# Issuing TensorE's row-spreading products twice in the edge stage of a graph layer

## The chip, the cores and the metric

The kernel runs on one core of a Trainium2 chip. The metric is device time in microseconds (us), from the first to the last instruction of one launch with what lies around it; lower is better.

## The reference

One hybrid graph layer on 3125 nodes of width 256 with 50000 edges: a typed attention over the edges, a linear-attention mixer and a gated feed-forward on half of the rows. The change touches only the first. Cut to what matters:

```python
K, Q, V = type_proj(xn, node_types, Wk/Wq/Wv)         # [3125, 8 heads, 32]
Ks, Qt, Vs = K[src], Q[tgt], V[src]                   # 50000 edges
for t in range(3):                                    # edge types
    scores = sum((Ks @ Wa[t]) * Qt, -1) / sqrt(32) * relation_pri[t]
    w = softmax(where(edge_type == t, scores, -inf), over all edges)
    msgs += where(edge_type == t, w * (Vs @ Wm[t]), 0)
agg = segment_sum(msgs, tgt)                          # edges are sorted by tgt
```

## The kernel before

A first stage projects keys, values and queries per node into DRAM tables. The second stage, which the change touches, walks over the edges. Edges are sorted by target; 128 x 4 of them are a **group** g (98 groups), and two groups are a **block** b (49 blocks). What follows is a third stage: the sums of the windows are joined, normalised and run through the feed-forward.

For a group, GpSimd issues four indirect DMAs that gather key and value rows by source (`rows_of`, L1415) into one of 7 slots (6 toward the end), and SyncE loads a window of 64 query rows for each half (`q_window`). The target rows are not gathered. ScalarE builds a transposed one-hot matrix `ohT` from the targets' keys (L1477, L1480), and TensorE spreads the window's rows to the edges with it (`target_rows`, L1615): for k in 0, 1 and for each half hg of the partitions one fp32 product of 64x128 with 64x256 into `qr_ps[g % 2]`, a buffer of two PSUM banks. Only the last product signals `qd`. The trace shows two matmul records for each fp32 product, so 8 records for a group. The products of a group wait until VectorE has read the same buffer two groups earlier (`at_least(pe, pr, g - 1)`).

VectorE multiplies the gathered keys by the spread rows (`products`, L1784) and sums them per head (`head_sums`, L1791); per block it subtracts a maximum (L1825), sums exponentials (L1832), adds the type mask (L1800), takes maxima (L1810), receives the turned maxima from TensorE (`maximum`, L1817) and weighs the gathered values (`messages`, L1841). TensorE sums the messages by target (`window_sums`, L1632), turns the sums (L1643), sums the exponentials (`totals`, L1653) and turns and spreads maxima (L1662, L1669). ScalarE copies (L1515, L1521), exponentiates (L1505) and builds the second one-hot matrix (L1492, L1496).

25 tiles of the mixer run in the same stage, two in every three blocks from block 7 to block 44: `mix_h` (L1685) on TensorE in the tile's block, a Gelu on ScalarE (L1537, with a table load), and in the next block `mix_y` (L1692, L1694) on TensorE and `mix_row` (L1927), statistics and gain on VectorE. So the blocks from 7 on come in threes: with `mix_h` alone (7, 10, ... 43), with both (8, 11, ... 41), with `mix_y` alone (9, 12, ... 42, and 44). In the blocks without `mix_y`, VectorE does two steps of a search for shared nodes instead (L1868 to L1885).

Every engine's order is written out by hand, and an engine works its queue strictly in that order. TensorE's order in block b is: `target_rows(2b+2)`, `turn_sums(2b-4)`, `mix_y` if any, `turn_sums(2b-3)`, `target_rows(2b+3)`, `totals(b-1)`, `mix_h` if any, `turn_maxima(b)`, `window_sums(2b-2)`, `spread_maxima(b)`, `window_sums(2b-1)`. VectorE's is: `products(2b)`, `head_sums(2b)`, `subtract(b-1)`, `products(2b+1)`, `mix_row` or a search step, `head_sums(2b+1)`, `weights(b-1)`, `mark(b)`, `maxima(b)`, `messages(2b-2)`, `maximum(b)`, `messages(2b-1)`, then the mixer's gain or a search step.

Of the kernel before, what the change touches and what calls it, by code (L numbers as in the profile page):

```python
# [95 lines left out]
def build(nc, a, out):  # L96
# [15 lines left out]
    with ExitStack() as ctx:  # L112
# [322 lines left out]
        def at_least(eng, event, count):  # L435
            if count > 0:
                eng.wait_ge(event, count)
# [58 lines left out]
        with nc.Block() as block:  # L496
# [862 lines left out]
            def in_range(g):  # L1359
                return 0 <= g < NG  # L1360
# [244 lines left out]
            def _(pe):  # L1605
                def target_rows(g):
                    if not in_range(g):
                        return
                    s = g % QRING
                    pe.wait_ge(oh, g + 1)  # L1610
                    pe.wait_ge(qin[s], 32 * (g // QRING + 1))
                    at_least(pe, pr, g - 1)
                    for k in range(2):
                        for hg in range(2):
                            ins = pe.matmul(qr_ps[g % 2][:, (2 * hg + k) * D:(2 * hg + k + 1) * D],  # L1615
                                            ohT[64 * hg:64 * hg + 64, g % 2, k * P:(k + 1) * P],
                                            qwin[64 * hg:64 * hg + 64, s, :], start=True, stop=True)
                    ins.then_inc(qd, 1)
# [80 lines left out]
                pe.wait_ge(s_end, 2)  # L1699
                pe.wait_ge(s_ed, 1)  # L1700
                target_rows(0)
                target_rows(1)
                for b in range(NB):
                    if b == SEARCH_AT - 2:
                        turn_bases(1)
                    target_rows(2 * b + 2)
                    turn_sums(2 * b - 4)
                    for m in mix_tiles(b, 1):
                        mix_y(m)
                    turn_sums(2 * b - 3)  # L1710
                    target_rows(2 * b + 3)
                    totals(b - 1)
                    for m in mix_tiles(b, 0):
                        mix_h(m)
                    turn_maxima(b)
                    if b < NB - 1:
                        window_sums(2 * b - 2)
                    spread_maxima(b)
                    if b < NB - 1:
                        window_sums(2 * b - 1)  # L1720
# [1044 lines left out]
```

## Time and profile before

| | us |
|---|---|
| median of 3 runs | 998.99 |
| lowest, highest | 997.55, 1001.36 |
| profiled execution, its own time | 997.39 |
| its span, first to last instruction | 995.6 |
| TensorE busy | 852.8 (86%) |
| VectorE busy | 781.2 (78%) |
| ScalarE busy | 607.7 (61%) |
| GpSimd busy | 597.5 (60%) |
| mean granted TensorE clock | 0.925 of full |

The shares are means over three stages with different limits. The edge stage lies between about 250 and 754 us of the span, and only there does the change act. The profile gives the stage's instructions by line; a busy time joins overlapping records, while "mean ns" is that of one record.

### The profile page before, as it was taken

How to read it: one execution, taken by the hardware profiler on the slowest of the kernel's cores; microseconds unless marked ns; L12 is line 12 of the kernel's file. 1: busy time of each engine (PE TensorE's matmuls, PEld its weight loads, DVE VectorE, ACT ScalarE, POOL GpSimd, SP SyncE). 2: the span in 40 equal slices, each digit the busy share in tenths (PEclk: the TensorE clock that was granted, in tenths of full speed). 3: DMA queues.
4: the chain of work that ended last, by engine and by line, in shares of the span. 5: the costliest groups of instructions: out<-in, count | busy, mean ns of one | idle time of the engine just before them, and what ended most of it. 6: DMA issues, size and time to landing. Idle time of an engine off the chain costs nothing.

```text
span 995.6 us, 18441 instructions
## 1 busy us (share of the span) xinstructions
PE 852.8 (86%) x5153; PEld 628.8 (63%) x5153; DVE 781.2 (78%) x1682; ACT 607.7 (61%) x1540; POOL 597.5 (60%) x745
## 2 busy tenths in 40 slices
PE   4999999995787878778888887888769989999998
PEld 3776777763454555455555555554438978888886
DVE  6855666761698999999999999999997886997542
ACT  2565676763475988888988889888753233332121
POOL 4704777776777777777777777776770245663000
PEclk9999999998587999999988889888879999999999
DMA  8922666666888888888888888887844833320012
GB/s 281 284 88 100 229 222 215 223 217 203 270 252 254 255 269 272 273 271 259 265 269 264 270 267 264 263 266 242 244 141 154 242 122 112 93 80 22 0 56 74
DMA packets 126204, 202.76 MB, mean 204 GB/s; under 512 B 19755, under 2 KB 94846, under 8 KB 126102
## 3 DMA queue, kind: packets, MB, share of 16 engines
q0 software_dynamic: 38992, 129.87, 40.6%
q1 hardware_dynamic: 76630, 61.86, 20.5%
q10 hardware_dynamic: 10480, 9.83, 3.0%
q8 instruction: 44, 0.72, 0.3%
q14 instruction: 58, 0.48, 0.2%
HBM read 160.50 MB, written 40.99 MB: 202 GB/s over the span
## 4 chain that ended last, share of the span: by engine, by line
PE 51%; DVE 13%; POOL 12%; ACT 12%; issue 9%; DMA 3%; DVEq 0%; ACTq 0%; SPq 0%; POOLq 0%
POOL big L1415 11%; PE ps L2455 9%; PE ps L2441 9%; PE ps L932 5%; PE ps L1632 4%; PE ps L1615 3%; ACT edge L1492 3%; DVE big L1841 3%; PE ps L2405 3%; PE ps L973 3%; PE ps L944 2%; PE ps L920 2%; ACT L1537 2%; DMA big<-kv_scratch,src_i 2%; DVE big L1784 2%
## 5 line engine op out<-in xcount | busy, mean ns | idle before, releaser
L1415 POOL DMA_INDIRECT big<-kv_scratch,src_i x392 | 371.9, 949 | 124.6 <-issue 116.7
L1615 PE MATMUL ps<-edge 64*128 64x256 f32 x784 | 130.9, 459 | 53.7 <-DVE big L1784 19.5
L1632 PE MATMUL ps<-big,edge 128*64 128x256 f32 x784 | 134.7, 475 | 34.7 <-DVE big L1841 34.5
L1615 PEld LDWEIGHTS ps<-edge 64*128 64x128 f32 x784 | 80.6, 216 | 95.1 <-issue 54.7
L1784 DVE TENSOR_TENSOR big<-big,ps 128x1024 f32<-128x1024 f32 x98 | 119.1, 1215 | 8.4 <-DMA big<-kv_scratch,src_i 6.6
L1791 DVE TENSOR_REDUCE ps<-big 128x32 f32<-128x1024 f32 x98 | 120.1, 1225 | 2.5
L1841 DVE TENSOR_TENSOR big<-big,ps 128x1024 f32<-128x1024 f32 x98 | 118.0, 1205 | 0.0
L1492 ACT ACTIVATE edge<-edge 128x64 f32<-128x64 f32 x392 | 103.8, 339 | 1.6
L1632 PEld LDWEIGHTS ps<-big,edge 128*64 128x64 f32 x784 | 56.7, 162 | 68.0 <-DVE big L1841 44.3
L2368 ACT ACTIVATE big<-ps,fb 128x256 f32<-128x256 f32 (+2 forms) x104 | 39.4, 461 | 87.9 <-PE ps L2441 87.9
L2455 PE MATMUL ps<-big 128*128 128x256 f32 (+1 forms) x400 | 90.2, 381 | 1.1 <-ACT big L2368 1.1
L2441 PE MATMUL ps<-big 128*128 128x256 f32 (+2 forms) x416 | 89.9, 373 | 0.6 <-ACT big L2355 0.6
L2441 PEld LDWEIGHTS ps<-big 128*128 128x128 f32 x416 | 76.1, 196 | 8.9 <-issue 0.8
L2455 PEld LDWEIGHTS ps<-big 128*128 128x128 f32 (+1 forms) x400 | 74.0, 188 | 11.9 <-issue 1.6
L1515 ACT ACTIVATE edge<-ps 128x256 f32<-128x256 f32 x98 | 35.6, 376 | 57.9 <-PE ps L1632 56.2
L1477 ACT ACTIVATE edge<-edge,iota_n 128x256 f32<-128x256 bf16 x98 | 49.0, 500 | 13.5 <-DMA edge<-key_scratch 13.2
L932 PE MATMUL ps<-big,edge 128*128 x120 | 57.2, 599 | 0.0
L1480 ACT ACTIVATE edge<-edge,ones 128x256 f32<-128x256 f32 x98 | 49.8, 508 | 10.5 <-PE ps L1615 1.7
L1496 ACT ACTIVATE edge<-edge,ones 128x256 f32<-128x256 f32 x98 | 49.8, 509 | 9.1 <-ACT edge L1492 0.4
L664 POOL DMA_INDIRECT edge<-xn_scratch,big x30 | 30.0, 1001 | 39.9 <-DMA xn_scratch<-big 24.0
L1228 DVE TENSOR_TENSOR edge<-ps,big 128x512 f32<-128x512 f32 x30 | 20.8, 692 | 36.3 <-PE ps L932 34.6
L2405 PE MATMUL ps<-bd_m,big 128*126 128x128 f32 (+1 forms) x396 | 45.1, 275 | 2.5 <-DVE big L2119 2.2
(348 smaller groups left out, 1730.5 us busy)
## 6 DMA issues: line engine op xcount, KB each, us to landing
edge<-q_scratch SPq DMA_DIRECT2D x196, 64.0 KB
big<-kv_scratch,src_i POOLq DMA_INDIRECT x392
edge<-key_scratch SPq DMA_DIRECT2D x98, 64.0 KB
agg_scratch<-big SPq DMA_DIRECT2D x16, 252.0 KB
xn_scratch<-big ACTq DMA_DIRECT2D x5, 640.0 KB, 4.2
mix_scratch<-big SPq DMA_DIRECT2D x25, 128.0 KB
mix_x_scratch<-big SPq DMA_DIRECT2D x25, 128.0 KB, 1.9
wmix<-mix_x_scratch ACTq DMA_DIRECT2D x25, 128.0 KB
```

Of the source, the lines that this page charges most:

```text
L932: ins = pe.matmul(ps[1][:, :], xgT[:, t.k, ch * P:(ch + 1) * P], wall[:, ds(ty, 1), ch, 0:2 * D].rearrange("p a o -> p (a o)"), start=(ch ...
L1415: pool.indirect_dma_start(kv_slots[s][:, k, :], None, kv_d[0:N, :], bass.IndirectOffsetOnAxis(ap=src_i[:, e:e + 1], axis=0)).then_inc(got[ ...
L1480: act.activation(ohT[:, g % 2, :], dist, ACT.Relu, bias=ones[:, 0:1], scale=-1.0).then_inc(oh, 1)
L1492: ins = act.activation(gap[:, 2 * k + hg, :], iota_m, ACT.Abs, bias=neg_key[:, e:e + 1])
L1615: ins = pe.matmul(qr_ps[g % 2][:, (2 * hg + k) * D:(2 * hg + k + 1) * D], ohT[64 * hg:64 * hg + 64, g % 2, k * P:(k + 1) * P], qwin[64 * h ...
L1632: ins = pe.matmul(sums_of(g)[64 * hg:64 * hg + 64, :], oneh[:, g % OHRING, k, hg * 64:hg * 64 + 64], kv_slots[s][:, 2 * hg + k, D:2 * D], ...
L1784: dve.tensor_tensor(k_rows, k_rows, qr_ps[g % 2].rearrange("p (k d) -> p k d", d=D), ALU.mult).then_inc(pr, 1)
L1791: dve.tensor_reduce(scr[:, g // 2 % 2, :].rearrange("p (h k) -> p k h", k=BT)[:, (g % 2) * EG:(g % 2 + 1) * EG, :], kv_slots[slot_of(g)][: ...
L1841: dve.tensor_tensor(v, v, wgt[:, g // 2 % 2, (g % 2) * EG * H:(g % 2 + 1) * EG * H] .rearrange("p (k h d) -> p k h d", h=H, d=1).to_broadc ...
L2405: ins = pe.matmul(ps[4 + ck % 4][0:n, ch * P:(ch + 1) * P], stg[k % 2][:, ch, t, at:at + n], bd_m[:, t, :], start=(t == 0), stop=(t == ETY ...
L2441: ins = pe.matmul(hslot[q % 2][:, j * GT * P:j * GT * P + w], fw1[:, ch, f * P:(f + 1) * P], cols[:, ch, at:at + w], start=(ch == 0), stop ...
L2455: ins = pe.matmul(ps[4 + t % 2][0:m, 0:D], fh[:, p % 2, f, at:at + m], fw2[:, f, :], start=(f == 0), stop=(f == FJ - 1))
```

## The change

In `target_rows`, the loop over k runs over `[0, 1]` once for groups 0 and 1, and over `[0, 1, 0, 1]` for the groups from 2 on. The second pass issues the same four products again with the same operands, into the same places of the same buffer; each starts a new sum, so the result is that of the first pass. `qd` is signalled by the last product of the second pass.

```diff
@@ target_rows(g)
                     at_least(pe, pr, g - 1)
-                    for k in range(2):
+                    for k in [0, 1] * (2 if g > 1 else 1):
                         for hg in range(2):
                             ins = pe.matmul(qr_ps[g % 2][:, (2 * hg + k) * D:(2 * hg + k + 1) * D],
                                             ohT[64 * hg:64 * hg + 64, g % 2, k * P:(k + 1) * P],
```

## Rows read from the trace of the kernel before

**Rows 1.** The page's costliest group: busy, mean ns | idle before it, its releaser.

```profile
L1415 POOL DMA_INDIRECT big<-kv_scratch,src_i x392 | 371.9, 949 | 124.6 <-issue 116.7
```

**Rows 2.** Busy by stretch: length; PE, PEld, DVE, ACT, POOL; clock, DMA share, GB/s.

```profile
350.00:400.00 50.00, 40.46 (x279) 26.84 (x279) 47.99 (x78) 43.84 (x110) 37.81 (x41) 0.97 0.86 268
...
534.74:565.32 30.58, 25.22 (x163) 16.23 (x163) 28.31 (x45) 26.12 (x65) 23.09 (x25) 0.89 0.86 264
```

**Rows 3.** Timeline of VectorE, blocks 28 to 30: start, us, what, idle before.

```profile
532.10 1.22 DVE L1784 TENSOR_TENSOR big<-big,ps 128x1024 f32<-128x1024 f32 x1
...
535.27 0.35 DVE L1825 TENSOR_TENSOR edge<-edge,ps 128x192 f32<-128x192 f32 x1 [0.69 <-ACT edge L1515]
535.54 1.21 DVE L1784 TENSOR_TENSOR big<-big,ps 128x1024 f32<-128x1024 f32 x1
...
540.36 0.27 DVE L1817 TENSOR_REDUCE mall<-ps 24x1 f32<-24x128 f32 x1
...
542.13 1.22 DVE L1784 TENSOR_TENSOR big<-big,ps 128x1024 f32<-128x1024 f32 x1
...
546.88 0.42 DVE L1927 TENSOR_TENSOR wmix<-ps,v_L_mix_b 128x256 f32<-128x256 f32 x1 [0.77 <-PE ps L1694]
...
550.63 0.27 DVE L1817 TENSOR_REDUCE mall<-ps 24x1 f32<-24x128 f32 x1
...
552.56 1.21 DVE L1784 TENSOR_TENSOR big<-big,ps 128x1024 f32<-128x1024 f32 x1
...
557.00 0.43 DVE L1927 TENSOR_TENSOR wmix<-ps,v_L_mix_b 128x256 f32<-128x256 f32 x1 [0.53 <-PE ps L1694]
...
562.68 1.22 DVE L1784 TENSOR_TENSOR big<-big,ps 128x1024 f32<-128x1024 f32 x1
```

**Rows 4.** Timeline of TensorE, blocks 29 and 30.

```profile
544.02 1.14 PE L1615 MATMUL ps<-edge 64*128 64x256 f32 x8 [1.11 <-ACT edge L1480]
545.09 0.44 PE L1643 MATMUL ps<-ident,edge 128*128 128x128 f32 x2
...
546.99 1.14 PE L1615 MATMUL ps<-edge 64*128 64x256 f32 x8
...
548.41 1.14 PE L1685 MATMUL ps<-wmix 128*128 128x128 f32 x8
549.63 0.33 PE L1662 MATMUL ps<-ident,edge 128*128 128x128 f32 x1
550.76 1.08 PE L1632 MATMUL ps<-big,edge 128*64 128x256 f32 x8 [0.80 <-DVE big L1841]
...
554.15 1.13 PE L1615 MATMUL ps<-edge 64*128 64x256 f32 x8 [0.96 <-ACT edge L1480]
...
560.89 1.98 PE L1632 MATMUL ps<-big,edge 128*64 128x256 f32 x8 [0.80 <-DVE big L1841]
...
565.25 2.08 PE L1615 MATMUL ps<-edge 64*128 64x256 f32 x8
```

**Rows 5.** Timeline of ScalarE: two table loads for the Gelu, blocks 28 and 29.

```profile
541.06 1.28 ACT L1537 ACT_TABLE_LOAD   x1
...
551.18 1.28 ACT L1537 ACT_TABLE_LOAD   x1
```

**Rows 6.** The chain that ended last: start, us, what.

```profile
342.09 1.22 DVE big L1784
...
343.45 1.14 PE ps L1615 x8
```

**Rows 7.** Timeline of VectorE: the same instruction in blocks 7 and 45.

```profile
329.99 0.27 DVE L1817 TENSOR_REDUCE mall<-ps 24x1 f32<-24x128 f32 x1
...
714.19 0.27 DVE L1817 TENSOR_REDUCE mall<-ps 24x1 f32<-24x128 f32 x1
```

**Rows 8.** Timeline of VectorE: waits for gathered rows, in blocks 6 and 22.

```profile
314.27 1.22 DVE L1784 TENSOR_TENSOR big<-big,ps 128x1024 f32<-128x1024 f32 x1 [2.34 <-DMA big<-kv_scratch,src_i]
...
474.44 1.22 DVE L1784 TENSOR_TENSOR big<-big,ps 128x1024 f32<-128x1024 f32 x1 [0.25 <-DMA big<-kv_scratch,src_i]
```

**Rows 9.** Timeline of both engines: the first turned maxima, in block 0.

```profile
262.40 0.47 PE L1662 MATMUL ps<-ident,edge 128*128 128x128 f32 x1
...
262.91 0.28 DVE L1817 TENSOR_REDUCE mall<-ps 24x1 f32<-24x128 f32 x1 [4.71 <-PE ps L1662]
```

## The prediction

> **What bounds the kernel now.** I read the page first, to see which engines are dear and where. GpSimd's gathers are its costliest group and almost never wait for another engine [rows 1]; the shares of the table show TensorE and VectorE fullest. The change acts on the edge stage alone, so the second view is busy time by stretch [rows 2]. In a stretch of the first half (350 to 400 us) VectorE is busy 47.99 of 50 us and the clock is 0.97; GpSimd gets through 41 gathers, one in 1.22 us, so 8 of them pace a block at 9.76 us. Over three blocks of the second half (30.58 us, 10.19 each) VectorE is busy 28.31, ScalarE 26.12, TensorE 25.22, and the clock is 0.89. No engine is full, yet VectorE is nearly so: its idle time, 2.27 us in three blocks, is what a change can add to or take from. The third view is the timeline of VectorE over these blocks, 28 to 30, which are the three kinds: with `mix_h` alone (call it A), with both (B), with `mix_y` alone (C) [rows 3]. It shows idle time of 0.69 us in A, behind ScalarE's copy, and of 0.77 and 0.53 us in B and C, where `mix_row` (L1927) waits for `mix_y`, which TensorE has queued behind the products of L1615. The timeline of TensorE [rows 4] shows how it comes to that, and what a low clock costs: `window_sums` takes 1.98 us at the end of C and 1.08 in B, the spreading 2.08 us after it and 1.14 elsewhere, levels of 1.2 and 2.4 GHz. The last view is ScalarE's: from one table load to the next 10.12 us [rows 5], a block of the kinds A and B filled with its work.
>
> VectorE's last view: it waits for gathered rows 2.34 us in block 6 and, for the last time among the mixer's blocks, 0.25 us in block 22 [rows 8]. So up to about there the gathers pace the stage (9.8 a block), later the chain over VectorE, TensorE and ScalarE does (10.2).
>
> **The change, part by part.** It removes nothing and moves nothing; it adds 4 products, so 8 matmul records and 8 weight loads, to each of 96 groups. The first pass of 8 starts at 544.02 and the next operation at 545.09 [rows 4], so a second pass costs 1.07 us of TensorE at the high clock; at the low one 2.08 is the record's length, about 2.0 start to start. That is 2.14 us a block, 103 us in all if nothing hid it. No transfer, copy or wait is added. The buffer is free already, since nobody reads it before `qd`, which the second pass delays.
>
> What lies behind the delay depends on the block. I take each block from the start of `products(2b)` (p) to the start of `products(2b+2)`. Where VectorE decides, the spreading starts 1.36 us after p [rows 6]; call that S.
>
> In **B** TensorE does the first spreading, a turn, then `mix_y`. Now `mix_row` starts at 546.88, 2.86 us after S at 544.02 [rows 3, 4], and it is already the one waited for. With a second pass it starts at S + 3.93 = p + 5.29. From there to the next p VectorE has 5.68 us of unbroken work (546.88 to 552.56), which gives 10.97. Then TensorE: the second spreading starts at S + 2.97 now, at S + 4.04 then, and lasts 2.14; `totals` and `mix_h` took 1.42 - 1.07 = 0.35 and 1.07 us (546.99, 548.41 and the 1.14 of L1685 less the overlap of 0.07) [rows 4]. So the maxima are turned at S + 7.60, and known 0.38 later (a record of 0.33 and a hand-over of 0.05; at the low clock the pair is 0.51 apart [rows 9]), at p + 9.34. VectorE is ready for them 3.75 us after `mix_row` (546.88 to 550.63), at p + 9.04. That adds 0.30: B takes 11.27.
>
> In **C** there is no `mix_h`, so the maxima are turned in time: 10.97. (With one pass the same sum gives 2.86 + 5.68 + 1.36 = 9.90, near the 9.76 of the gathers: the two paces lie close together now.)
>
> In **A** no `mix_y` stands between. VectorE's own work from p to p is 542.13 - 532.10 - 0.69 = 9.34. The second spreading waits for `products(2b+1)`, which starts at p + 2.75 (535.54 less 532.10 less 0.69), so it starts at p + 4.11, lasts 2.14, and with the same 1.42 and 0.38 the maxima are known at p + 8.05. VectorE is ready at p + 7.57 (540.36 less 532.10 less 0.69). A takes 9.34 + 0.48 = 9.82. The first copy hides here behind VectorE's own work.
>
> The three sum to 32.06, against 30.58. This holds at the high clock throughout; TensorE would be busy some 28 of 32 us. I take the high clock, because the clock now falls at the end of C, after `mix_h` is missing and TensorE has stood idle in several pieces, and those pieces are just what the second passes fill. ScalarE doesn't come to bind: its 10.12 us fit in A plus B (21.1) and B, and with no table loads C leaves it several us.
>
> From block 7 to block 45 there are 38 blocks, 13 of kind A, 12 of B and 13 of C (44 counted there): 13 x 9.82 + 12 x 11.27 + 13 x 10.97 = 405.5 us. They take 714.19 - 329.99 = 384.2 us now [rows 7]. That is +21.3. It is more than 12.7 times 1.48, since the first half runs at the gathers' 9.8 us and loses that cover.
>
> Before block 7: in block 0 VectorE waits 4.71 us for the maxima behind two spreadings at the low clock [rows 9], and two second passes put up to 4 us there. Behind it stands the wait of 2.34 us for rows in block 6 [rows 8], which uses up part of that. I take +1, with bounds of 0 and +2. Past block 45 no `mix_y` stands between; the copies hide as in A, and a `window_sums` at the high clock is shorter by 1.98 - 1.08 = 0.90 [rows 4]: -1 for one such in four blocks, as an estimate. Sum: +21.
>
> The profiled execution took 997.39 (span 995.6), the median of the runs is 998.99. So the execution would read about 1018, the median 1020.
>
> **A rule that speaks against this.** The rows show the clock low after a C and high after two busier blocks. The Trainium skill, TensorE: Matmul & The Clock Gate, section "HAM oscillation — how this bites in real kernels", says that pauses between bursts of matmuls send the clock to half speed again and again, and that a kernel gains by keeping TensorE busy. By that rule the second passes would be a means to gain. The fall of the clock to half agrees with the trace (1.98 against 1.08 us). The rival below prices it from rows.
>
> **The rivals.**
> *The clock pays for the copies: faster.* If the products kept the clock high and cost nothing on the path, blocks 23 to 44 would go at the gathers' 9.76 us for 10.19: 22 x 0.43 = 9.5 us less, 990. It decides if the second pass costs under about 0.3 us in front of `mix_row`: B and C then take 10.97 - 0.77 = 10.20, A 9.34, and the 38 blocks 376 us, 8 less than now. For it speaks the clock of 0.89 [rows 2]; against it that `mix_row` waits for TensorE even in the blocks at the high clock [rows 3], and that two such waits of 1.31 us (p + 5.29 against VectorE ready at p + 3.98, which is 546.88 - 0.77 - 542.13) exceed all of the 2.27 us that VectorE idles now.
> *The copies are half hidden: no change.* If the records of a second pass overlapped those of the first, at 0.5 us a pass B and C would take 10.4, A 9.3: 381 us, 3 less than now, and 995. Nothing in the rows shows two such passes back to back cheaper than their sum.
> *The clock still falls at the end of each C.* Then A starts with two passes at the low clock, 4 us for 2.14, the second spreading starts 1.9 us later than counted, and A takes about 11.9. That is 2.1 x 13 = 27 more, 1047. For it: the clock falls now exactly there.
> *TensorE becomes the bound in every block*, 2.14 us on each of 48: 1102. Against it: idle time of 1.11 and 0.80 us within a block [rows 4].
>
> **How the numbers follow.** The likeliest case, slower by the waits in B and C, has 0.80; the clock still falling 0.08; TensorE the bound 0.01; half hidden 0.06; faster by the clock 0.05. A measurement of this kernel tells about 0.5%, 5 us. Slower 0.88 (part of the half-hidden case falls there too, and part of the first in the middle), same 0.07, faster 0.05. The range: below, without the turned maxima's 0.30 and 0.48 (-10) and with 0 before block 7, less 2 for a shorter second pass, 1007; above, a clock that falls in about half of the C blocks, or ScalarE late by 0.4 us in each block, 1034.
>
> **What would show it.** L1927's idle time of 0.77 and 0.53 us should grow to about 1.3 in B and C, released by `mix_y` (L1694); L1817 should show new waits of 0.3 to 0.5 us for L1662; the three blocks should take about 32.1; the clock in the edge stage should be near 1.0 and the waits for gathered rows after block 7 gone. L1615 should have 1552 records. The prediction is wrong if the clock stays at 0.89, if L1927's wait doesn't grow, or if blocks of kind A go past 10 us.

## The result and the profile after

The changed kernel takes 1005.96 us (median of 4 runs, 1003.36 to 1006.22), the kernel before 998.49 beside it: ratio 1.0065, 95% interval 1.0037 to 1.0094. Timed a second time, on another occasion, the ratio was 1.0049 (1.0026 to 1.0073). It is slower, as forecast, but by 7 us and not by 21; the stated range began at 1007.

Of the page of the changed kernel, the costliest group of TensorE and that of the window sums:

```profile
span 1004.2 us, 19977 instructions
...
L1615 PE MATMUL ps<-edge 64*128 64x256 f32 x1552 | 199.1, 396 | 49.9 <-DVE big L1784 25.3
...
L1632 PE MATMUL ps<-big,edge 128*64 128x256 f32 x784 | 113.2, 412 | 21.4 <-DVE big L1841 20.5
```

The window sums on the page of the kernel before:

```profile
L1632 PE MATMUL ps<-big,edge 128*64 128x256 f32 x784 | 134.7, 475 | 34.7 <-DVE big L1841 34.5
```

The span grew by 8.6 us (995.6 to 1004.2). L1615 has twice its records but for two groups (784 to 1552). Nothing in `window_sums` was changed, yet its mean record takes 412 ns where it took 475: more of them run at the high clock.

Busy time of the stretch from block 7 to the place where block 45 stood before, 384 us, first the kernel before, then the changed one:

```profile
330.00:714.00 384.00, 311.74 (x2026) 202.85 (x2026) 358.20 (x572) 328.85 (x820) 287.07 (x304) 0.91 0.85 263
```

```profile
330.00:714.00 384.00, 339.97 (x2583) 249.51 (x2583) 348.71 (x559) 327.85 (x805) 281.69 (x298) 1.00 0.84 259
```

TensorE is busy 28 us more, VectorE gets through 559 instructions where it had done 572, and the granted clock is 1.00 where it was 0.91. Who VectorE waits for in this stretch, before and after (us in total, times, longest):

```profile
DVE wmix L1927 <- PE ps L1694: 11.4, 21, 0.8
DVE edge L1825 <- ACT edge L1515: 7.1, 12, 0.7
DVE big L1784 <- DMA big<-kv_scratch,src_i: 3.0, 7, 1.0
```

```profile
DVE wmix L1927 <- PE ps L1694: 30.6, 25, 1.4
DVE mall L1817 <- PE ps L1662: 0.9, 1, 0.9
```

These rows account for VectorE's idle time in the stretch: they sum to 21.5 us before and 31.5 after, and VectorE is busy 9.5 us less. `mix_row` waits 19.2 us more for `mix_y`. In return the wait of `subtract` behind ScalarE's copy (7.1 us), which came from window sums at the low clock, is gone, and so is that for gathered rows (3.0).

The timeline of VectorE over three blocks of the changed kernel, of the kinds B, C and A, to be laid beside [rows 3]:

```profile
549.68 1.22 DVE L1784 TENSOR_TENSOR big<-big,ps 128x1024 f32<-128x1024 f32 x1
...
554.76 0.42 DVE L1927 TENSOR_TENSOR wmix<-ps,v_L_mix_b 128x256 f32<-128x256 f32 x1 [1.21 <-PE ps L1694]
...
558.51 0.27 DVE L1817 TENSOR_REDUCE mall<-ps 24x1 f32<-24x128 f32 x1
...
560.44 1.21 DVE L1784 TENSOR_TENSOR big<-big,ps 128x1024 f32<-128x1024 f32 x1
...
571.19 1.22 DVE L1784 TENSOR_TENSOR big<-big,ps 128x1024 f32<-128x1024 f32 x1
```

And that of TensorE, to be laid beside [rows 4]:

```profile
551.04 2.00 PE L1615 MATMUL ps<-edge 64*128 64x256 f32 x16 [0.60 <-ACT edge L1480]
552.97 0.44 PE L1643 MATMUL ps<-ident,edge 128*128 128x128 f32 x2
...
554.87 2.00 PE L1615 MATMUL ps<-edge 64*128 64x256 f32 x16
...
557.16 1.14 PE L1685 MATMUL ps<-wmix 128*128 128x128 f32 x8
558.13 0.27 PE L1662 MATMUL ps<-ident,edge 128*128 128x128 f32 x1
...
568.27 0.33 PE L1662 MATMUL ps<-ident,edge 128*128 128x128 f32 x1 [0.22 <-DVE edge L1810]
569.40 1.08 PE L1632 MATMUL ps<-big,edge 128*64 128x256 f32 x8 [0.80 <-DVE big L1841]
...
575.20 2.00 PE L1615 MATMUL ps<-edge 64*128 64x256 f32 x16
```

B takes 10.76 us (549.68 to 560.44), C 10.75, A 9.36 (the three together take 30.87, from one L1817 at 547.90 to its third successor at 578.77, less 21.51). Forecast were 11.27, 10.97 and 9.82. `mix_row` starts 3.72 us after the spreading (551.04 to 554.76), not 3.93; then come 5.68 us to the next products, and 1.36 to the next spreading, both as read before. No wait of L1817 is listed in any of the three. At the end of C the window sums take 1.08 us: the clock held.

So a burst of 16 records lasts 1.93 us start to start (551.04 to 552.97) where one of 8 lasted 1.07. The second pass costs 0.86. Taken in very short stretches, the timeline gives the records by pairs, one of each half of the partitions. From the timeline of TensorE in the changed kernel (the start is what counts, the rest joins neighbours):

```profile
551.04 0.49 PE L1615 MATMUL ps<-edge 64*128 64x256 f32 x2 [0.60 <-ACT edge L1480]
551.34 0.63 PE L1615 MATMUL ps<-edge 64*128 64x256 f32 x4
...
552.63 0.41 PE L1615 MATMUL ps<-edge 64*128 64x256 f32 x2
552.97 0.33 PE L1643 MATMUL ps<-ident,edge 128*128 128x128 f32 x1
```

From the second pair to the eighth it is 1.29 us, so the pairs follow each other by 0.215. But the first is followed by the second only after 0.30, and the last by the next operation after 0.34. A burst of n pairs so lasts n x 0.215 plus 0.21 once. For n = 4 that is 1.07, for n = 8 it is 1.93. The 0.21 is a price of going into and out of the burst, and a second pass behind the first doesn't pay it again.

### The profile page after: what moved, and what is told of

It is laid out like the page before. It is cut to its first block, busy times and chain, and to the rows that moved or that the text cites. A ratio compares the mean times of both kernels' runs of the same rounds, so it can differ in the third digit from the quotient of the medians.

```text
span 1004.2 us, 19977 instructions
## 1 busy us (share of the span) xinstructions
PE 894.5 (89%) x5921; PEld 692.8 (69%) x5921; DVE 779.6 (78%) x1682; ACT 613.8 (61%) x1540; POOL 597.6 (60%) x745
## 4 chain that ended last, share of the span: by engine, by line
PE 54%; DVE 22%; ACT 8%; issue 7%; POOL 6%; DMA 3%; DVEq 0%; ACTq 0%; POOLq 0%
PE ps L2455 9%; PE ps L2441 8%; PE ps L1615 8%; DVE big L1841 6%; POOL big L1415 5%; PE ps L932 5%; DVE big L1784 4%; PE ps L2405 3%; DVE ps L1791 3%; PE ps L973 3%; ACT edge L1492 2%; PE ps L944 2%; PE ps L920 2%; PE ps L1692 2%; DMA big<-kv_scratch,src_i 2%
## 5 line engine op out<-in xcount | busy, mean ns | idle before, releaser
L1615 PE MATMUL ps<-edge 64*128 64x256 f32 x1552 | 199.1, 396 | 49.9 <-DVE big L1784 25.3
L1615 PEld LDWEIGHTS ps<-edge 64*128 64x128 f32 x1552 | 156.0, 191 | 85.3 <-issue 53.5
L1632 PE MATMUL ps<-big,edge 128*64 128x256 f32 x784 | 113.2, 412 | 21.4 <-DVE big L1841 20.5
L1632 PEld LDWEIGHTS ps<-big,edge 128*64 128x64 f32 x784 | 49.7, 142 | 50.4 <-DVE big L1841 31.0
L1521 ACT ACTIVATE big<-ps 128x252 f32<-128x252 f32 x98 | 34.5, 376 | 20.1 <-PE ps L1643 19.3
```

The source lines that it names most:

```text
L1632: ins = pe.matmul(sums_of(g)[64 * hg:64 * hg + 64, :], oneh[:, g % OHRING, k, hg * 64:hg * 64 + 64], kv_slots[s][:, 2 * hg + k, D:2 * D], ...
```

## The experiments

Times are medians; "b7 to b45" is the time between L1817 in block 7 and in block 45, 384.2 us before [rows 7] and 391.98 after (330.49 to 722.47). It is read from the one profiled execution of each kernel, which can lie off the median: it took 1015.14 us in the first experiment below and 991.41 in the fifth. The theory (T) was: the loss is the price of one extra pass, 0.86 us, in front of `mix_row` in each block with `mix_y`, and part of it is paid back by a clock that stays high.

**Only the first spreading of a block doubled.**

```diff
-for k in [0, 1] * (2 if g > 1 else 1):
+for k in [0, 1] * (2 if g > 1 and g % 2 == 0 else 1):
```

> Only the first spreading of a block (even groups), the one in front of mix_y, is doubled; the second is single. Theory T (the slowdown is the price of one extra pass, 0.86 us, in front of mix_row in the blocks with mix_y; the clock stays high): blocks with mix_y keep 10.76 us, the others 9.34, so the time stays that of the changed kernel, 1006 (1003 to 1009), and L1927 keeps its wait of 1.2 us. Rival U (each copy costs the same wherever it stands, 96 copies for 7.5 us): half of the loss, 1002. Rival V (the second copies are what holds the clock): the clock falls again at the end of each block without mix_h, about 1 us in three blocks more: 1015 to 1020.

Measured: 1022.59 us, ratio 1.0243 (1.0207 to 1.0280); b7 to b45 403.87. With half of the copies it is slower than with all. The clock is 0.94 over the stretch of 384 us: 1.00 up to 440 us, 0.92 behind, where it falls at the end of C again:

```profile
572.00 0.33 PE L1662 MATMUL ps<-ident,edge 128*128 128x128 f32 x1 [1.08 <-DVE edge L1810]
...
574.47 1.71 PE L1632 MATMUL ps<-big,edge 128*64 128x256 f32 x8
576.28 2.92 PE L1615 MATMUL ps<-edge 64*128 64x256 f32 x16
...
586.48 2.00 PE L1615 MATMUL ps<-edge 64*128 64x256 f32 x16 [1.51 <-ACT edge L1480]
```

The spreading of 16 records that starts A at the low clock takes 2.92 us, and the one that starts B waits 1.51 us for ScalarE's one-hot matrix, late by the same delay. U is refuted, and T's main branch too: I had expected the first copies alone to hold the clock. It is rival V that came nearest; the median lies 2.6 us above its window, and the clock falls behind 8 of the 12 C blocks, not behind 9, 12, 15 and 39. It shows both effects at once: the loss in front of `mix_row` (31.8 us of waiting in the stretch) with no clock to pay for it.

**Only the second spreading doubled.**

```diff
-for k in [0, 1] * (2 if g > 1 else 1):
+for k in [0, 1] * (2 if g > 1 and g % 2 == 1 else 1):
```

> Only the second spreading of a block (odd groups), behind mix_y, is doubled. Theory T: mix_row waits 0.4 to 0.8 us as in the kernel before, a block with mix_y takes 1.36 + 2.86 + 5.68 = 9.90 us, ScalarE holds one of three at 10.1 and the gathers pace at 9.76; if the clock stays high three blocks take about 29.5 us instead of 30.58 and the time is 988 to 992, faster than both. If 48 copies aren't enough for the clock: about 998, as before. Rival U: 1002.

Measured: 993.72 us, ratio 0.9938 (0.9916 to 0.9959), faster than both; b7 to b45 380.53, granted clock 0.99. `mix_row`'s waits, all for L1694, fall to 7.7 us in the stretch, and the gathers come out as a limit:

```profile
DVE wmix L1927 <- PE ps L1694: 7.7, 23, 0.4
DVE big L1784 <- DMA big<-kv_scratch,src_i: 7.1, 12, 1.1
DVE mall L1817 <- PE ps L1662: 3.3, 2, 1.7
```

It is 2 us slower than T's window, which took the gathers at 9.76 us a block (their pace is read in the fifth experiment). Its blocks take 9.75 and 9.89 us for long, with two of 12: after a wait for rows in front of the second product TensorE idles 1.80 us, and its next burst runs at the low clock (3.30 us for 16 records).

```profile
505.33 3.30 PE L1615 MATMUL ps<-edge 64*128 64x256 f32 x16 [1.80 <-DVE big L1784]
...
509.22 1.16 PE L1685 MATMUL ps<-wmix 128*128 128x128 f32 x8
```

**Three passes.** `[0, 1] * (3 if g > 1 else 1)`.

> Three passes for every group from the third on. Theory T by the same hand sum with 0.86 us a pass: mix_row at S + 4.58 and the maxima late by 0.86 in a block with mix_y and mix_h (12.5 us), 11.6 with mix_y alone, maxima late by 1.7 with mix_h alone (11.0): 35.1 us for three blocks against 30.9, so about 1060 (1050 to 1068). Rival U (cost in proportion to the copies): 1013.

Measured: 1057.31 us, one run; b7 to b45 442.04. From products to products B takes 12.43 us, C 11.62 and A 10.95, 35.00 together against the 35.1 of the hand sum. The cost is far from proportional to the copies: the first extra pass costs 7 us, the second 51, because there is no more clock to win back (1.00) and TensorE is now late with the maxima too:

```profile
649.04 0.28 DVE L1817 TENSOR_REDUCE mall<-ps 24x1 f32<-24x128 f32 x1 [1.63 <-PE ps L1662]
...
656.76 0.42 DVE L1927 TENSOR_TENSOR wmix<-ps,v_L_mix_b 128x256 f32<-128x256 f32 x1 [2.08 <-PE ps L1694]
```

**The changed kernel with `mix_y` ahead of the first spreading.**

```diff
-                    target_rows(2 * b + 2)
-                    turn_sums(2 * b - 4)
                     for m in mix_tiles(b, 1):
                         mix_y(m)
+                    target_rows(2 * b + 2)
+                    turn_sums(2 * b - 4)
                     turn_sums(2 * b - 3)
```

> The changed kernel (two passes) with mix_y put ahead of the first spreading on TensorE. Theory T: mix_row no longer waits behind the passes, L1927's idle time is about 0, three blocks take 29.3 to 29.7 us (ScalarE's 10.1 and the gathers' 9.76 are next), the clock stays high: 987 to 992. Rival U (TensorE's load as such costs): 1006, with the wait moved to another instruction. Rival W (mix_y ahead delays the spreading, which is late next): L1784 waits for L1615 and it gains less than 5 us, 1001 or more.

Measured: 993.80 us, ratio 0.9939 (0.9915 to 0.9963); b7 to b45 381.54. The same products as in the changed kernel, and 12 us less: L1927 has no wait left. The load as such (U) isn't what costs. It misses T's 992 by 2 us, since VectorE now waits 11.0 us for gathered rows in the stretch and 9.7 for maxima.

**The same order with single passes.** The edit above, made to the kernel before.

> The kernel before (one pass) with mix_y put ahead of the first spreading. It separates the two effects. Theory T: VectorE's waits of 0.5 to 0.8 us in front of mix_row go, but nothing holds the clock, which still falls about once in three blocks (0.92 to 0.95 in the edge stage); ScalarE's 10.1 us and the low clock keep three blocks at about 30: 992 to 998. Rival C (the clock is all that the extra passes gave in the runs that were faster): no gain without them, 998 or more. Rival W (only the wait matters, the clock nothing): as fast as the same order with two passes or faster, 989 to 993.

Measured: 994.67 us, ratio 0.9938 (0.9921 to 0.9954); b7 to b45 380.14, clock 0.91. VectorE's waits in the stretch:

```profile
DVE big L1784 <- DMA big<-kv_scratch,src_i: 11.2, 17, 1.3
DVE edge L1825 <- ACT edge L1515: 6.7, 12, 0.8
DVE mall L1817 <- PE ps L1662: 0.3, 1, 0.3
```

The waits before `mix_row` are gone, that for ScalarE's copy has stayed, the clock is as low as before, and the time is that of the two-pass kernel in this order. T's window (992 to 998) is met, with a clock a little lower than it said. C is refuted: a high clock isn't needed for 994. In this order it isn't worth anything that shows either, which is rival W's claim, though the time lies 2 us above W's window. GpSimd tells why. A gather waits for L1632 when the window sums have not yet freed its slot. Such waits in the stretch, first before, then after, then here, where the fixed pause ("issue") stands above them:

```profile
POOL big L1415 <- PE ps L1632: 6.4, 6, 3.8
```

```profile
POOL big L1415 <- PE ps L1632: 17.0, 18, 4.7
```

```profile
POOL big L1415 <- issue: 91.4, 300, 0.3
POOL big L1415 <- PE ps L1632: 2.6, 8, 0.5
```

And its timeline here:

```profile
599.98 0.95 POOL L1415 DMA_INDIRECT big<-kv_scratch,src_i  x1 [0.30 <-issue]
601.23 0.95 POOL L1415 DMA_INDIRECT big<-kv_scratch,src_i  x1 [0.30 <-issue]
```

A gather that waits for no other engine starts 1.25 us behind the one ahead of it, so 8 of them take 10.0 us, and 38 blocks 380. Here GpSimd hardly ever waits for a slot (2.6 us), and 380.14 is that pace: whatever else is freed, VectorE spends it waiting for rows.

**Both means**: the new order, second spreading doubled.

> mix_y ahead of the first spreading, and only the second spreading of a block doubled: both means at once. Theory T: the chain would allow about 29.2 us for three blocks, but the gathers pace at 9.76 a block (29.3) and a wait for them lets TensorE pause and the clock fall; so hardly better than either means alone: 988 to 994. A rival by which the two gains add up (5 us each below the kernel before): 984 to 987.

Measured: 994.24 us, ratio 0.9936 (0.9913 to 0.9959); b7 to b45 380.28. T's 994 is met but for 0.2 us, and the gains don't add. Three kernels, with the clock at 0.91, 0.98 and 0.99, end within 1.5 us of each other in this stretch.

**Copies in the second spreading of the C blocks only.**

```diff
-for k in [0, 1] * (2 if g > 1 else 1):
+for k in [0, 1] * (2 if g % 2 == 1 and g > 1 and mix_tiles((g - 3) // 2, 1)
+                   and not mix_tiles((g - 3) // 2, 0) else 1):
```

> Only the second spreading in the blocks with mix_y alone is doubled, 12 or 13 copies in all. Theory T: it fills TensorE just ahead of the place where the clock falls in the kernel before, so the clock holds in most groups of three blocks and the time is 990 to 996. If the clock is held only by more passes than these: 997 to 1001.

Measured: 995.58 us, ratio 0.9944 (0.9923 to 0.9964); b7 to b45 379.52, clock 0.96. T's window is met. A dozen copies, ahead of the place where the clock used to fall, do nearly what 48 did.

**As many copies as the changed kernel, elsewhere**: the second pass of an even group goes behind `mix_y`, and `qd` is signalled there.

```diff
-                    target_rows(2 * b + 2)
+                    first_pass(2 * b + 2)
                     turn_sums(2 * b - 4)
                     for m in mix_tiles(b, 1):
                         mix_y(m)
+                    second_pass(2 * b + 2)
```

> As many copies as the changed kernel, at another place: the first pass of an even group stays in front of mix_y, its second pass goes behind mix_y (qd is signalled there). Theory T: with the same load on TensorE the wait in front of mix_row shrinks to 0.4 to 0.8 us; the maxima are known about as late as VectorE is ready for them, plus 0.2 to 0.5; three blocks take 29.3 to 30: 989 to 998. Rival U (the number of extra products decides): 1006 as the changed kernel.

Measured: 1001.22 us, ratio 1.0013 (0.9990 to 1.0035): no loss against the kernel before timed beside it (1001.19), but 3 us outside T's window; b7 to b45 388.87, clock 1.00. (The 384.2 us before come from an execution of 997.39 us, fast for a kernel whose median was 1001.19 here.) Timeline of TensorE in a B block (L1609 is here the product, L1656 the turn, L1707 the end of `mix_y`):

```profile
581.30 1.14 PE L1609 MATMUL ps<-edge 64*128 64x256 f32 x8
582.37 0.44 PE L1656 MATMUL ps<-ident,edge 128*128 128x128 f32 x2
```

```profile
581.41 0.42 DVE L1941 TENSOR_TENSOR wmix<-ps,v_L_mix_b 128x256 f32<-128x256 f32 x1 [0.36 <-PE ps L1707]
586.31 0.28 DVE L1831 TENSOR_REDUCE mall<-ps 24x1 f32<-24x128 f32 x1 [1.06 <-PE ps L1675]
```

`mix_row` (L1941) waits 0.36 us again. A second pass that stands alone costs 1.07 (581.30 to 582.37), since it pays for going in and out. VectorE waits 1.06 us for the maxima, not the 0.2 to 0.5 that I had written. Only a small part of that is the 0.21. `mix_row` now starts 4.23 us after the products (577.18), where it started 5.08 after them in the changed kernel, so VectorE is ready for the maxima 0.85 us sooner, while TensorE has as many products ahead of them as there. What was freed in front of `mix_row` is lost again at the maxima.

**Half a second pass.** `for k in [0, 1] if g < 2 else [0, 0, 1]`.

> Half of a second pass: only the two products for k = 0 are issued twice (order 0, 0, 1), in every group from the third on. Theory T (a product pair has a pitch of 0.213 us, whatever a whole burst pays on top at its start and end once): a burst lasts 1.07 + 0.43 = 1.50 us start to start, mix_row waits about 0.8 us, a block with mix_y takes 1.36 + 3.29 + 5.68 = 10.33 us, the one without 9.34 to 9.5, three blocks 30.0 to 30.2 if the clock is held: 994 to 1000, about as the kernel before or a little faster. Rival (an extra burst has a fixed price of its own, so half a pass costs nearly as much as a whole): 1003 to 1006. If half a pass doesn't hold the clock: 1002 to 1010 with about 11 us for the block that starts at the low clock.

Measured: 1001.82 us, ratio 1.0004 (0.9986 to 1.0022), above T's 1000 by 2 us, and b7 to b45 387.17. The changed kernel timed beside it:

> The changed kernel itself, on the same chip as the half pass, so that the two can be set side by side: 1004 to 1008, three blocks 30.87 us.

1004.53 us, ratio 1.0049 (1.0026 to 1.0073). The burst and the wait behind it, from the timelines of TensorE and VectorE with half a pass:

```profile
558.61 1.57 PE L1615 MATMUL ps<-edge 64*128 64x256 f32 x12 [0.73 <-DVE big L1784]
560.10 0.44 PE L1643 MATMUL ps<-ident,edge 128*128 128x128 f32 x2
...
568.23 1.98 PE L1632 MATMUL ps<-big,edge 128*64 128x256 f32 x8
570.13 2.75 PE L1615 MATMUL ps<-edge 64*128 64x256 f32 x12
```

```profile
561.89 0.43 DVE L1927 TENSOR_TENSOR wmix<-ps,v_L_mix_b 128x256 f32<-128x256 f32 x1 [0.78 <-PE ps L1694]
```

The burst takes 1.49 us (558.61 to 560.10), 0.42 over the single one; `mix_row`'s wait is 0.78 in C; blocks B and C take 10.2 to 10.3. The price per pair holds (0.215; the 0.213 above is read a little low). But half a pass doesn't hold the clock every time: it is 0.95 in the stretch, and falls here at the end of C, as behind 3 of the 12 C blocks.

## Why the prediction was wrong

**The step that failed** is the size of two terms of the sum. The first is "so a second pass costs 1.07 us of TensorE at the high clock". That is the distance from the start of a burst of one pass to the next operation. It holds 0.86 us that grow with the records and 0.21 that are paid once per burst. The second pass, behind the first, costs 0.86. With that, `mix_row` starts at S + 3.72, and B and C take 1.36 + 3.72 + 5.68 = 10.76 but for the maxima. A doubled burst lasts 1.93 and not 2.14. So in B the maxima come 0.42 us earlier, with VectorE ready 0.21 earlier, which makes 0.09 of the forecast wait of 0.30; in A they come 0.21 earlier, which makes 0.27 of 0.48. The 38 blocks then take 13 x 9.61 + 12 x 10.85 + 13 x 10.76 = 395.0, which is +10.8 and not +21.3, and the time would be 1010, inside the stated range. This is 10.5 us of the error.

The second term is what was left of the turned maxima, 4.3 us. They were forecast to be late by 0.30 in B and 0.48 in A. No wait of L1817 is listed in B, and in A the 9.36 us leave about 0.1 for it. `mix_h` had been counted at 1.07 us, a record less a guessed overlap; start to start it takes 0.97 (557.16 to 558.13), and so it did in the kernel before:

```profile
538.68 1.14 PE L1685 MATMUL ps<-wmix 128*128 128x128 f32 x8
539.66 0.27 PE L1662 MATMUL ps<-ident,edge 128*128 128x128 f32 x1
```

In A the second spreading starts at p + 4.01 (571.19 to 575.20), not at p + 4.11, and the maxima are received 0.31 us behind their turn (578.46 to 578.77), not 0.38. With A at 9.36 and B and C at 10.76 the blocks take 390.7, +6.5, and the time would be 1005. Measured were 391.98, 0.8 of the rest in block 19, behind one fall of the clock. The range went wrong in the same place: its lower end took the maxima away, but gave only 2 us for a shorter second pass, where 25 x 0.21 = 5.3 were due in front of `mix_row`. The half, whole, double and single-standing extra pass (burst 1.49, 1.93, the 35.00 us of three blocks, and 1.07) bear the split of the price out.

**Where the added time goes** was right: the first pass's copy stands in front of `mix_y`, `mix_row` waits for that, and almost nothing else of VectorE does. Its wait rose from 11.4 to 30.6 us, and with `mix_y` moved ahead the loss was gone. That the first copy hides in A was right too.

**The clock stays high** was right (0.91 to 1.00), and the reason given, idle pieces filled late in C, fits the traces. In C of the kernel before, TensorE idles 0.86 to 1.07 us in front of the turned maxima, and the clock falls behind 9 of 12 such blocks. With the first copies alone the piece stays at 1.08, since the late `mix_row` makes VectorE's maxima late as well: 8 of 12. With half a pass it is 0.66, and 3 of 12; with both copies, or the second alone, 0.22, and 1 of 12. What I hadn't seen is that only the copies behind `mix_y` shorten it, and that a dozen of them are enough (0.22, and 2 of 12). That this piece is the cause is not shown: with the first copies the same 1.08 stood in C blocks 9 and 12, and the clock held.

**The rival that the clock pays** named a price of 0.3 us in front of `mix_row` as the point from which it decides. With the true 0.86 there it came out slower; with no copy there, the kernel was faster: 993.7 us, where the rival had 990 with the gathers at 9.76. The rule of the Trainium skill, "HAM oscillation — how this bites in real kernels" in TensorE: Matmul & The Clock Gate, is that pauses bring the clock down and a kernel gains by keeping TensorE busy. The traces agree in that filling raised the clock (0.91 to 1.00, 0.99 and 0.96). That the kernel gains by it held for 993.7 and 995.6 us, and not for 1006 and 1022.6, where the filling stood in front of `mix_y`.

**The gathers as the next limit** I had priced too low. I divided 50 us by the 41 gathers counted in it, 1.22; from start to start it is 1.25, in the kernel before too, which makes 10.0 us a block and 380 for the 38 blocks, less at most the few us that GpSimd may be ahead at the start. The kernel before stood only 4 us above that. All five faster kernels stop there, at 379.5 to 381.5 us in their profiled executions, whatever their clock. The windows of T for the second, fourth and sixth experiment were worked out with 9.76, and all three lay too low. Whether a faster issue of the gathers would carry the time further wasn't tried.

**The ends**: before block 7, +0.5 (forecast +1); from block 45 to 48, -0.4 (29.38 against 29.80; forecast -1); behind block 48 0.7 us more, not forecast. The second profile of the changed kernel has -0.6 before block 7, so amounts of this size are scatter from one execution to the next.

## What to carry to other kernels

Price added work of an engine by the pitch of its records, not by the length of the whole burst: what a burst pays at its ends is paid once, and a repetition behind it doesn't pay it again, while one put elsewhere does. Where a product's order on TensorE puts it ahead of something that VectorE waits for, moving that something ahead took the whole wait away here, with one pass and with two, and costs no instruction. If idle TensorE time lets the clock fall, fill it where nobody waits behind the filling. And before pricing a gain, take the pace of the engine that works without waiting from start to start: it says how much any change to the others can bring, here 4 us of the stretch.

## What the runs showed of the hardware that was not expected

Pairs of 64x256 products, one on each half of the partitions, follow by 0.215 us at the high clock; the burst costs another 0.21 us in all at its two ends, in bursts of 8, 12 and 16 records alike. Indirect gathers on GpSimd that waited for no other engine started 1.25 us apart, 0.95 busy and 0.30 between them.

Over the stretch of 384 us the clock was 1.00 with TensorE busy 340 us, and 0.91 with 312, where it fell behind 9 of 12 C blocks. With 320 to 322 it was 0.94 when the copies stood in front of `mix_y`, 0.99 when they stood behind it, and 0.91 with no copies and `mix_y` moved ahead; with 311 it was 0.96, a dozen copies behind `mix_y`. So the place of the work counts, not its sum alone. Busy time is itself shorter at the high clock, so these sums are not amounts of work.
